# Moving the gate's softmax of a mixture-of-experts layer from the token tiles to the expert phase

## The reference

```
logits = xf @ gate_w.T                      # 32 for each token
scores = softmax(logits)
tw, ti = top_k(scores, 4)
tw = tw / (tw.sum(-1) + 1e-20)              # the four weights
y = sum over the four: tw * expert(ti)(xf)
```

## Time and profile before

| | busy us | share |
|---|---|---|
| PE | 777.2 | 89% |
| PEld | 639.1 | 73% |
| DVE | 593.4 | 68% |
| POOL | 482.0 | 55% |
| ACT | 469.4 | 54% |

### The profile page before, as it was taken

One profiled execution on the slowest core, in us unless ns is written; L12 is line 12 of the kernel. 1 busy time (PEld: TensorE's weight loads), 2 busy tenths in 40 slices (PEclk: granted clock), 3 DMA queues, 4 the chain that ended last, 5 costly groups with the idle time before them and its releaser, 6 DMA issues.

```text
span 876.3 us, 22261 instructions
## 1 busy us (share of the span) xinstructions
PE 777.2 (89%) x6034; PEld 639.1 (73%) x6035; DVE 593.4 (68%) x2017; ACT 469.4 (54%) x1411; POOL 482.0 (55%) x684
## 2 busy tenths in 40 slices
PE   4899999999999999632999999999999999999995
PEld 2566666666666666422898998899899898888884
DVE  2578888888888888540565666566566566477887
ACT  2678888888888888411444444444444443322331
POOL 0126566666666666570455555555555556576665
PEclk9999999999999999855999999999999999999998
DMA  6345655555555555776344444344344342577875
GB/s 193 101 121 168 177 168 172 178 169 178 175 167 169 172 172 178 236 193 180 116 132 127 123 129 130 121 127 131 120 127 131 120 130 98 189 247 236 257 243 179
DMA packets 101889, 142.01 MB, mean 162 GB/s; under 512 B 16171, under 2 KB 83043, under 8 KB 101219
## 3 DMA queue, kind: packets, MB, share of 16 engines
q1 hardware_dynamic: 87395, 101.18, 39.3%
q0 software_dynamic: 14080, 38.89, 12.7%
q10 hardware_dynamic: 384, 1.58, 0.7%
HBM read 86.73 MB, written 58.82 MB: 166 GB/s over the span
## 4 chain that ended last, share of the span: by engine, by line
PE 39%; DMA 4%; issue 4%; DVE 3%; POOL 2%; SPq 1%; POOLq 0%; DVEq 0%; ACT 0%
PE bank L1197 9%; PE bank L1205 8%; PE bank L1219 6%; PE bank L1221 6%; PE bank L1230 4%; PE bank L1212 4%; DMA got<-yt_d 2%; DVE acc L1394 2%; DMA x2t<-xn2t_d 1%; PE bank L1268 1%; PE bank L1248 1%; POOL scaled L1330 1%; PE bank L1259 1%; PE bank L1255 1%; DVE wts L1399 1%
## 5 line engine op out<-in xcount | busy, mean ns | idle before, releaser
L1319 POOL DMA_INDIRECT yt_d<-yo,name_i x160 | 157.7, 986 | 28.7 <-issue 22.5
L740 POOL DMA_INDIRECT xs_d<-rgu,sloti x128 | 127.5, 996 | 41.7 <-issue 31.6
L1197 PE MATMUL bank<-down_w,rdt 128*128 x320 | 97.7, 387 | 19.8 <-issue 18.7
L1364 DVE TENSOR_TENSOR h<-bank,gated 128x176 f32<-128x176 f32 x160 | 54.7, 342 | 86.8 <-ACT gated L1283 86.8
L1317 POOL TENSOR_TENSOR fence<-ones 128x1 f32<-128x1 f32 x160 | 29.4, 184 | 140.6 <-DVE name_i L1354 140.4
L1205 PEld LDWEIGHTS bank<-ht,rd_w 88*128 88x128 f32 x640 | 96.7, 192 | 8.2 <-issue 0.3
L1279 ACT ACTIVATE rdt<-bank 128x128 f32<-128x128 f32 x160 | 44.3, 277 | 104.6 <-PE bank L1205 104.5
L1205 PE MATMUL bank<-ht,rd_w 88*128 88x128 f32 x640 | 97.7, 275 | 0.0
L1283 ACT ACTIVATE gated<-bank 128x176 f32<-128x176 f32 x160 | 50.7, 317 | 87.1 <-PE bank L1221 87.1
L1353 DVE COPY yo<-bank 128x256 f32<-128x256 f32 x160 | 67.3, 420 | 26.0 <-PE bank L1197 25.9
L1359 DVE COPY ht<-bank 88x256 f32<-88x256 f32 x160 | 67.3, 420 | 21.4 <-PE bank L1212 12.2
(11 more groups left out here) (163 smaller groups left out, 1928.0 us busy)
## 6 DMA issues: line engine op xcount, KB each, us to landing
xg<-xs_d SPq DMA_DIRECT2D x160, 128.5 KB, 2.1
got<-yt_d SPq DMA_DIRECT2D x32, 512.0 KB, 4.2
raw<-in_raw SPq DMA_DIRECT2D x32, 496.0 KB
v<-v SPq DMA_DIRECT2D x128, 34.0 KB, 2.0
xs_d<-in_spare SPq DMA_DIRECT2D x4, 1028.0 KB, 7.4
xin<-in_x SPq DMA_DIRECT2D x32, 128.0 KB
ctxt<-in_ctxt SPq DMA_DIRECT2D x32, 128.0 KB, 3.9
xres<-in_x SPq DMA_DIRECT2D x32, 128.0 KB
```

Of the source, the lines that this page charges most:

```text
L740: nc.gpsimd.indirect_dma_start(xs_d, bass.IndirectOffsetOnAxis(sloti[:, b, k:k + 1], 0), rgu[:, b, k, :], None)\
L1197: nc.tensor.matmul(y_ps[b], rdt[:, b, :], weight(down_w, DOWN), start=True, stop=True)\
L1319: nc.gpsimd.indirect_dma_start(yt_d, bass.IndirectOffsetOnAxis(name_i[:, b, :], 0), yo[:, b, :], None)\
```

## The change

The five instructions of the gate's softmax that stood in each token tile (two on ScalarE, and three on VectorE that turn the sums into weights) are removed. In their place GpSimd copies each tile's 32 logits, as a product with ones, into a tensor for all 32 tiles, and VectorE, in place of the negated maximum, copies the four largest. In the expert stage VectorE subtracts the maximum for all tiles at once in step 2, ScalarE does two Exp in step N + 4, and VectorE sums, divides and writes all weights in step N + 5. The copy of logits into `rgl` (L720) waits in addition for GpSimd's copy of the tile two before.

```
 # ScalarE, token tile, step s, i = s - 5
-act.wait_ge(ntop_done, i + 1)
-nc.scalar.activation(egate[:, b, :], rgl[:, b, DIM:DIM + EXPERTS], ACT.Exp, bias=ntop[:, b, :],
-                     accum_out=zsum[:, b, 0:1]).then_inc(gexp_done, 1)
-nc.scalar.activation(etop[:, b, :], top8[:, b, 0:TOPK], ACT.Exp, bias=ntop[:, b, :],
-                     accum_out=zsum[:, b, 1:2]).then_inc(gexp_done, 1)
 # ScalarE, ahead of the copy into rgl
+    act.wait_ge(logits_kept, i - 1)
 # GpSimd, token tile, between xrb and scatter(s, ph, 1, TOPK)
+i, b = s - 5, (ph - 5) % 2
+if live(i, TILES):
+    pool.wait_ge(rgu_done, i + 1)
+    nc.gpsimd.tensor_tensor(col(logits, i), rgl[:, b, DIM:DIM + EXPERTS], ones[:, 0:EXPERTS],
+                            ALU.mult).then_inc(logits_kept, 1)
 # VectorE, token tile
-nc.vector.tensor_scalar(ntop[:, b, :], top8[:, b, 0:1], -1.0, None, ALU.mult).then_inc(ntop_done, 1)
+nc.vector.tensor_copy(col(top4, i), top8[:, b, 0:TOPK])
-gate_weights(s, ph)          # L949, L953, L955 with their waits
 # ScalarE, expert stage
+if isinstance(s, int) and s == N + 4:
+    act.wait_ge(gsub_done, 2)
+    nc.scalar.activation(logits[:, :, :], logits[:, :, :], ACT.Exp).then_inc(gexp_done, 1)
+    nc.scalar.activation(etop[:, :, :], etop[:, :, :], ACT.Exp).then_inc(gexp_done, 1)
 # VectorE, expert stage
+if isinstance(s, int) and s == 2:
+    # logits - top1 (128x1024) and etop = top4 - top1 (128x128), each .then_inc(gsub_done, 1)
...
+if isinstance(s, int) and s == N + 5:
+    dve.wait_ge(gexp_done, 2)
+    nc.vector.tensor_reduce(zsum[:, 0, :], logits[:, :, :], AX.X, ALU.add).then_inc(gsum_done, 1)
+    nc.vector.tensor_reduce(zsum[:, 1, :], etop[:, :, :], AX.X, ALU.add).then_inc(gsum_done, 1)
+    dve.wait_ge(gsum_done, 2)
+    # scalar_tensor_tensor, reciprocal (128x32 each), product into weights (128x128), a wait between each
...
```

More of the change, by code:

```diff
@@ L143, in build @@
         weights = sb("weights", [P, TILES, TOPK])
+        logits = sb("logits", [P, TILES, EXPERTS])
+        top4 = sb("top4", [P, TILES, TOPK])
         bank03 = ps("bank03", [P, 4, 512])
@@ L218, in build @@
             rgl = asb("rgl", [P, 2, DIM + EXPERTS])
-            ntop = asb("ntop", [P, 2, 1])
             top8i = asb("top8i", [P, 2, 8], U32)
             topif = asb("topif", [P, 2, TOPK])
[L222 to L225, removed]
             chosen = asb("chosen", [P, 2, TOPK, EXPERTS])
@@ L275, in build @@
                 asem(n) for n in ("ln2_st", "ln2_mv", "ln2_ve", "ln2_rstd", "xn2_done", "x2t_psum", "x2t_done"))
-            rgu_psum, rgu_done, top_done, ntop_done, topi_done, topif_done, gexp_done, wden_done = (
-                asem(n) for n in ("rgu_psum", "rgu_done", "top_done", "ntop_done", "topi_done",
-                                  "topif_done", "gexp_done", "wden_done"))
+            rgu_psum, rgu_done, logits_kept, top_done, topi_done, topif_done = (
+                asem(n) for n in ("rgu_psum", "rgu_done", "logits_kept", "top_done", "topi_done", "topif_done"))
             chosen_done, member_done, r_psum, rowof_done, picked_done, slotf_done, sloti_done, free_done = (
@@ L941, in choose @@
                                                     AX.X, ALU.max).then_inc(member_done, 1)
[L943 to L955, removed]
                     def residual(s, ph):
@@ L1082, in build @@
             name_f = esb("name_f", [P, AHEAD, 1])
+            etop = esb("etop", [P, TILES, TOPK])
+            zsum = esb("zsum", [P, 2, TILES])
+            wden = esb("wden", [P, 2, TILES])
             name_i = esb("name_i", [P, RING, 1], I32)
@@ L1096, in build @@
             N = ETILES
+            gsub_done, gexp_done, gsum_done, wden_done, weights_done = (
+                esem(n) for n in ("gsub_done", "gexp_done", "gsum_done", "wden_done", "weights_done"))
             TURN, UP, HTURN, RDOWN, DOWN, LAG = 3, 5, 7, 9, 11, 12
@@ L1371, in expert @@
                             nc.vector.tensor_copy(name_f[:, b, :], xg[:, b, DIM:ROW]).then_inc(name_done, 1)
+                        if isinstance(s, int) and s == 2:
+                            top1 = top4[:, :, 0:1]
+                            nc.vector.tensor_tensor(logits[:, :, :], logits[:, :, :],
+                                                    top1.broadcast_to([P, TILES, EXPERTS]),
+                                                    ALU.subtract).then_inc(gsub_done, 1)
+                            nc.vector.tensor_tensor(etop[:, :, :], top4[:, :, :],
+                                                    top1.broadcast_to([P, TILES, TOPK]),
+                                                    ALU.subtract).then_inc(gsub_done, 1)
+                        if isinstance(s, int) and s == N + 5:
[3 more added lines that the diff above has]
+                            dve.wait_ge(gsum_done, 2)
+                            nc.vector.scalar_tensor_tensor(out=wden[:, 0, :], in0=zsum[:, 0, :], scalar=1e-20,
+                                                           in1=zsum[:, 1, :], op0=ALU.mult, op1=ALU.add)\
+                                .then_inc(wden_done, 1)
+                            dve.wait_ge(wden_done, 1)
+                            nc.vector.reciprocal(wden[:, 1, :], wden[:, 0, :]).then_inc(wden_done, 1)
+                            dve.wait_ge(wden_done, 2)
+                            nc.vector.tensor_tensor(weights[:, :, :], etop[:, :, :],
+                                                    wden[:, 1, :].unsqueeze(2).broadcast_to([P, TILES, TOPK]),
+                                                    ALU.mult).then_inc(weights_done, 1)
+                            dve.wait_ge(weights_done, 1)
                     run_experts(dve, expert)
```

## The result

The kernel after takes 887.24 us (median; 885.24 to 887.87), the kernel before 877.38 (875.43 to 878.13): a ratio of 1.0117 with the interval 1.0093 to 1.0141, slower by 9.9 us. They are single executions, and the one after is the fastest of its four.

A forecast was written before the change was run, and what follows sets the result against it. The prediction took a ring of GpSimd's and VectorE's halves to bound the token step. From the profiled 878.0 us, 7.3 (copy) + 2.9 (end of experts) - 0.3 (end of token tiles) gave 887.9, stated as 888, range 880 to 897.

The forecast's parts named there:

- The ring: Token step: GpSimd sets 6.05 us from L892 to L974, VectorE 4.84 us from L974 to L892, together 10.89 us.
- the copy: Token steps: GpSimd's added 128x32 product, inside its closed run, costs 0.27 us a step, 7.3 us over 27 steps.
- the end of the experts: After the last silu: table switch, Exp and sums delay the last expert stores by 2.9 us.
- The dear copy: Rival, token steps: copy held by VectorE's L900 or as costly as 128x256, 17.0 to 19.4 us; chance 0.13.
- the hidden one: Rival, token steps: the copy vanishes in GpSimd's issue gaps between scatters, costing 0 there, 880.6 us in all; chance 0.11.
- The removal: Token tiles: softmax work taken from VectorE (0.81 us a step) and ScalarE (0.58 us) is worth 0.
- the rival by which one of them sets the step (863): Token stage: VectorE or ScalarE is the bound, 17.8 us gained, 863 us in all; chance of the faster case 0.09.
- VectorE's half: Token step from L974 to the next L892: 4.84 us, set by VectorE, where its changes lengthen or shorten the step.
- The wait of L974: Token step, VectorE waiting for GpSimd's power L772: a sign of being right, up from 0.47 to about 1.4 us.
- The page's figure: Table switch at the end of the experts: the skill's 1.38 us drain, not used; it would make the sum 889.2.
- The start of the experts: Two VectorE subtractions, over by about 409.2 before its first need at 411.24: 0, or 1.5 us without that cover.
- the token drain: End of the token tiles: the last tiles lose 0.81 us on VectorE; taken as -0.3 us, between -0.8 and 0.

The follow-up runs named there:

- e1: The changed kernel with GpSimd's copy of the logits put ahead of rqk instead of behind xrb: 884.1 us, 1.0076 to the kernel before.
- e3: The kernel before with its softmax kept, plus GpSimd's copy of the logits behind xrb and ScalarE's wait for it: 883.22 us, ratio 1.0065.
- e4: The kernel before without the gate's softmax in the token tiles, weights set to 0.25: 878.45 us, ratio 1.0011.
- e5: The kernel before with xrb moved from behind rqk to the start of the token step: 867.13 us, ratio 0.9879.
- e10: The changed kernel with nothing moved and half of TensorE's key and value products left out: 883.71 us, 1.0073 to the kernel before.
- e2: The changed kernel with both Exp and VectorE's sums and weights in step 2 of the expert stage: 885.26 us, 1.0096 to the kernel before.
- e6: The changed kernel with xrb and the copy of the logits at the start of the token step: 870.96 us, 0.9926 to the kernel before.
- e8: The kernel before with xrb at the step's start and half of TensorE's key and value products left out: 861.88 us, ratio 0.9808.

## Why the prediction was right

The forecast was 888.0 and the median is 887.24. The ring that it rests on held in e1, e3, e4, e5 and e10, each of which could have shown it false; that xrb, taken out of GpSimd's run, gives time back (e5) shows best that this run sets the step. That the total came within 1 us is partly luck: the copy was priced 1.5 us too high, the loop's turn (1.0) was missing, the end of the experts was 0.2 too low, and these nearly cancel. The interval of the measured difference, 8.2 to 12.4 us, is wider than any of them.

**The copy**: forecast 0.27 us a step, 7.3 in all. Its duration was on the line, 242 ns for 249. A step grew by 0.21 to 0.22 (e3, where it is alone), 5.8 in all. The dear copy and the hidden one both fell: it takes 240 to 264 ns in every step, and the gap behind it didn't shrink. ScalarE's new wait cost nothing that shows. The steps average 10.99 us ("about 11.0" was the sign of being right) for 10.73.

**The removal**: forecast 0, and e4 shows 0.5 (interval -0.7 to 2.6). VectorE's and ScalarE's time did turn into waiting, and the rival by which one of them sets the step (863) fell. What the forecast did not have is the loop's turn, 0.11 us more in every second step, of which 0.07 to 0.08 show in the step: 13 x 0.08 = 1.0 us. It stands in VectorE's half, where the prediction said that every change counts.

**VectorE's half** is not VectorE's alone, as the prediction has it. In the kernel before it also waits for GpSimd in there, for the power of the first norm (60 to 345 us):

```profile
DVE xn L835 <- POOL rstd L753: 8.0, 24, 0.4
```

That is 0.33 us in each steady step, before and after alike, so the forecast lost nothing by it. But a change to this power, too, would count.

**The wait of L974** was to rise from 0.47 to about 1.4 and rose to 1.19 (in this step). VectorE's mean came 4.60 us after the mean square (213.69 against 209.09) instead of 4.37, with the longer copy and conversions beside GpSimd; all of that lies under the wait.

**The end of the experts**: forecast 2.9 (its terms add up to 2.8: 752.2 against 749.36), measured 3.1, and e2 gives it back. The order of events came as told, table load, Exp, sums, the held result of a tile, the hole in the stores. The Exp on 1024 columns took 1.06 (1.15 taken), VectorE's part 2.4 us (749.95 + 0.29 - 747.89) as assumed. The second table load is hidden, as forecast.

**The page's figure.** ScalarE: Activation LUTs, in the Trainium skill, section "What ACT_TABLE_LOAD costs", adds a drain of 1.38 us to each load. At the load before the batch this trace shows none: it starts 0.01 us behind the silu and the Exp starts 0.02 us behind it. The row was the right price.

**The start of the experts and the token drain** can't be told from nothing: the handover differs more from trace to trace than the 0.3 us that the prediction took off.

**The sum.** 5.8 + 1.0 + 3.1 = 9.9, beside 9.9 in the medians; an agreement to 0.1 us is more than these runs can show. In the profiled pair the steps give 5.6, since an early step that is not yet steady was 0.5 us shorter after. What failed was not in the prediction but in the expectation of e6: it took GpSimd's shortened run from the step in full, though VectorE's own way to the mean and the power behind it is nearly as long, and the way through TensorE and ScalarE to the scores is, too.

## What to carry to other kernels

Work is only worth taking off an engine where that engine ends a wait; here the list of waits said so (VectorE waits for GpSimd in each step) while the busy shares of 83 to 97% said nothing about it. The cheap copy that made the batch possible was put into the one closed run of the slower engine; 0.24 us at the wrong place, 27 times, cost more than the whole softmax was worth. Before counting on a gain from shortening one way round a ring, measure the other ways: here one through VectorE and one through TensorE and ScalarE stood only 0.2 to 0.3 us behind. And a run that takes work off an engine without effect clears that piece of work, not the engine: look where its time went as waiting.

## What the runs showed of the hardware beyond that

The gap in which VectorE turns its loop was 0.26 us in every kernel with the softmax in the tile (before, e3, e5, e8) and 0.37 in every one without it (after and all others). Which property of the instruction list does it is open; no run isolates it. VectorE's copy of four columns takes 0.40 and 0.17 us in turn in the steady steps of e6 and 0.17 in all of e1, where the negated maximum of one column always took 0.15. A scatter on GpSimd overlaps it in the short cases as well as in the long, so that alone is not the cause; it was not tried either.
